# Graph network, residual layers and four norms on one core: opening and ending re-ordered, two norms of the ending moved to ScalarE

## The reference

```
for _ in range(3):                                  # L0: gated graph network, in_mat = out_mat = adj
    a  = adj @ h ; av = [a, a]
    z  = sigmoid(lin(av, w3) + lin(h, u3)) ; r = sigmoid(lin(av, w4) + lin(h, u3))
    hv = tanh(lin(av, w5) + lin(r * h, u5))
    h  = (1 - z) * h + z * hv
x = ln(x + h)                                       # norm 0
rel = adj.T * (x Wq)(x Wk)^T ; rel = rel / ||rel||  # L1: relation between nodes
x = ln(x + rel @ (x Wv))                            # norm 1
x = ln(x + (adj @ x) @ weight2 + bias2)             # L2, norm 2
x = ln(x + norm_adj @ (x @ weight3) + bias3)        # L3, norm 3
```

## Time and profile before

| | us |
|---|---|
| median of 3 runs | 1214.63 (1214.09 to 1214.99) |
| the profiled execution | 1214.77 |
| its span in the trace | 1212.9 |
| PE busy in the span | 1198.3 (99%) |
| DVE busy | 1002.6 (83%) |
| ACT busy | 655.7 (54%) |
| POOL busy | 191.7 (16%) |

### The profile page before, as it was taken

How to read it: one execution, slowest core, us unless ns; L and a number is a source line. 1 busy time by engine, 2 the same in 40 slices (tenths; PEclk the granted TensorE clock), 3 DMA queues, 4 the chain that set the end, 5 groups by cost and what they waited for, 6 DMA issues and landing times.

```text
span 1212.9 us, 21243 instructions
## 1 busy us (share of the span) xinstructions
PE 1198.3 (99%) x7454; PEld 1079.2 (89%) x7454; DVE 1002.6 (83%) x2220; ACT 655.7 (54%) x1179; POOL 191.7 (16%) x447
## 2 busy tenths in 40 slices
PE   9999999999999999999999999999999999999997
PEld 8789899898988989899898998989889898998896
DVE  7689788897878879788897888978789797885898
ACT  5455555555555555555555555555555555554442
POOL 1002021110211203012020211102111030120022
PEclk9999999999999999999999999999999999999998
DMA  6030221303113030220302213031130302200001
GB/s 209 18 88 18 70 71 35 104 0 88 50 35 104 0 104 35 52 87 14 107 17 69 69 35 104 0 87 52 35 104 0 104 35 51 87 12 24 1 2 35
DMA packets 105021, 66.93 MB, mean 55 GB/s; under 512 B 65690, under 2 KB 98468, under 8 KB 104996
## 3 DMA queue, kind: packets, MB, share of 16 engines
q1 hardware_dynamic: 104784, 66.08, 18.2%
q0 software_dynamic: 192, 0.52, 0.2%
q10 hardware_dynamic: 20, 0.01, 0.0%
HBM read 35.13 MB, written 23.07 MB: 48 GB/s over the span
## 4 chain that ended last, share of the span: by engine, by line
PE 97%; DVE 2%; POOL 0%; ACT 0%; issue 0%; DVEq 0%; POOLq 0%
PE b_ps L520 41%; PE f_ps L520 32%; PE f_ps L515 15%; PE b_ps L515 7%; PE f_ps L682 1%; PE b_ps L746 1%; PE b_ps L564 0%; PE f_ps L1057 0%; DVE f_stats L1683 0%; DVE hf_feat L1699 0%; DVE f_gate L1699 0%; DVE b_rh_lo L1725 0%; PE b_ps L579 0%; DVE b_ps L1720 0%; PE f_ps L589 0%
## 5 line engine op out<-in xcount | busy, mean ns | idle before, releaser
L428 POOL TENSOR_TENSOR b_var_eps<-b_moments,eps 128x2 f32<-128x2 f32 x120 | 34.7, 289 | 904.2 <-DVE b_moments L1690 904.2
L1120 ACT ACTIVATE f_cand<-f_ps,bias_c 128x512 f32<-128x512 f32 x66 | 45.4, 689 | 85.2 <-PE f_ps L520 85.2
L430 POOL TENSOR_TENSOR b_rstd<-b_var_eps,neg_half 128x2 f32<-128x2 f32 x120 | 88.0, 733 | 9.4
L1068 ACT ACTIVATE b_rh_hi<-b_ps 128x512 fp32r<-128x512 f32 x90 | 53.6, 596 | 63.0 <-PE b_ps L520 62.9
L1108 ACT ACTIVATE f_gate<-f_ps,bias_r 128x512 f32<-128x512 f32 x66 | 45.3, 686 | 71.0 <-PE f_ps L520 71.0
L1068 ACT ACTIVATE b_a_hi<-normed 128x512 fp32r<-128x512 f32 x60 | 37.8, 630 | 60.0 <-DVE normed L1699 60.0
L520 PE MATMUL f_ps<-adjT_hi,hf_node_hi 128*128 128x256 f32 x264 | 66.4, 285 | 0.0
L520 PE MATMUL f_ps<-adjT_lo,hf_node_hi 128*128 128x256 f32 x264 | 65.0, 280 | 0.0
L1582 DVE TENSOR_TENSOR f_cand<-f_z,f_cand 128x512 f32<-128x512 f32 x66 | 45.4, 688 | 23.0 <-ACT f_cand L1120 22.9
L1725 DVE TENSOR_TENSOR b_rh_lo<-b_ps,b_rh_hi 128x512 fp32r<-128x512 f32 x90 | 61.1, 679 | 4.0 <-ACT b_rh_hi L1068 3.9
L1566 DVE TENSOR_TENSOR f_gate<-f_gate,hf_feat 128x512 f32<-128x512 f32 x66 | 44.7, 678 | 20.0 <-ACT f_gate L1108 20.0
(11 more groups left out here) (340 smaller groups left out, 4304.4 us busy)
## 6 DMA issues: line engine op xcount, KB each, us to landing
x_front<-in_x SPq DMA_DIRECT2D x16, 512.0 KB, 3.9
x_blocks<-in_x SPq DMA_DIRECT2D x60, 128.0 KB, 2.9
input_t<-hf_feat SPq DMA_DIRECT2D x15, 512.0 KB, 3.0
turn_sum<-normed SPq DMA_DIRECT2D x14, 512.0 KB, 2.7
result<-turn_sum SPq DMA_DIRECT2D x56, 128.0 KB, 2.9
turn_f<-f_gate SPq DMA_DIRECT2D x14, 512.0 KB, 2.7
f_z<-turn_f SPq DMA_DIRECT2D x56, 128.0 KB, 2.8
out<-result SPq DMA_DIRECT2D x14, 512.0 KB, 3.2
```

Of the source, the lines that this page charges most:

```text
L428: pool.tensor_tensor(Y.var_eps[:, g], Y.moments[:, g, :, 1], eps[:], ALU.add).then_inc(Y.s_var, 1)
L430: pool.tensor_tensor(Y.rstd[:, g], Y.var_eps[:, g], neg_half[:], ALU.pow).then_inc(Y.s_rstd, 1)
L1068: return act.activation(dst, src, ACT.Copy)
L1120: act.activation(L.cand[:, k], L.ps1[:, k], ACT.Tanh, bias=bias_c[:, k:k + 1]).then_inc(L.s_tanh, 1)
```

## The change

The loop's `body` is as it was. Four things are changed.

1. **First back state, turned in the back lane's bank.** `turn_h(state_b, 0, k)` wrote `front.ps1`; it now writes `back.ps1` (`turn_bank`), and waits for `s_prep_lo` 8 (the preparation that used that bank). The mix of pair 1's first round, `mix(front, 2, k, 1)`, no longer waits for the turned state to be read, but for the tanh of the round before that reads the same bank, and stands ahead of the turning.
2. **Norms 1 and 2 of the ending on ACT.** `normalise` and the copy `conv_x_hi` go; ACT computes `x * rstd + shift` twice, once into `x_hi` (`layer_x_hi`) and once into the full-precision tile (`layer_normed`), from SBUF for norm 1 and from PSUM for norm 2. `conv_x_lo` and `fill` wait for the second. POOL adds `neg_mean` and `shift` for these norms.
3. **The hand-written orders of `start()`** on all engines.
4. **The hand-written orders of `finish()`**, with norm 3 of one graph applied ahead of the last statistics.

```diff
@@ norms
         def shifts(q, j, g):
-            return 8 * q + (4 if j == 3 else 0) + 2 * g + 2
+            return 8 * q + (4 if j >= 2 else 0) + 2 * g + 2
...
+        def turn_bank(S, v):
+            return back.ps1 if S is state_b and not later(v) else front.ps1
...
@@ POOL
             def inverse_std(Y, q, j, g, ending=False):
-                shifted = j in (0, 3) and not ending
+                shifted = j in ((1, 2) if ending else (0, 3))
...
@@ PE
-                if pair is not None and later(pair):
+                if pair is not None and isinstance(n, int) and n == 2:
+                    pe.wait_ge(front.s_tanh, upto(1, k))
+                elif pair is not None and later(pair):
                     pe.wait_ge(state_b.s_node_lo, upto(pair - 1, k))
...
             def turn_h(S, v, g):
                 pe.wait_ge(S.s_feat, upto(v))
-                turn(front.ps1, g, S.feat, S.s_turned)
+                if S is state_b and not later(v):
+                    pe.wait_ge(s_prep_lo, 8)
+                turn(turn_bank(S, v), g, S.feat, S.s_turned)
...
@@ PE, start()
                 candidate_reset(front, 1, 1)
+                for k in range(2):
+                    mix(front, 2, k, 1)
+                for k in range(2):
+                    turn_h(state_b, 0, k)
                 base(back, 0, 0)
                 for k in range(2):
-                    turn_h(state_b, 0, k)
+                    mix(back, 0, k, turned=True)
                 base(back, 0, 1)
...
@@ ACT
+            def layer_x(Y, q, j, g, dst):
+                for c in range(C):
+                    src = Y.normed[:, g, c] if j == 1 else Y.ps0[:, g, c * D:(c + 1) * D]
+                    last = act.activation(dst[:, g, c], src, ACT.Identity, bias=Y.shift[:, g, c:c + 1],
+                                          scale=Y.rstd[:, g, c:c + 1])
+                return last
+
+            def layer_x_hi(Y, q, j, g):
+                act.wait_ge(Y.s_shift, shifts(q, j, g))
+                layer_x(Y, q, j, g, Y.x_hi).then_inc(Y.s_x_hi, 1)
+
+            def layer_normed(Y, q, j, g):
+                act.wait_ge(Y.s_shift, shifts(q, j, g))
+                act.wait_ge(Y.s_x_hi, conv(q, j - 1, g))
+                layer_x(Y, q, j, g, Y.normed).then_inc(Y.s_normed, 1)
...
@@ DVE
-            def conv_x_lo(Y, q, j, g):
+            def conv_x_lo(Y, q, j, g, ending=False):
+                if ending:
+                    dve.wait_ge(Y.s_normed, mid(q, j + 1, g))
                 graph_lo(Y.x_lo, Y.x_hi, Y.normed[:, g], Y.s_x_hi, conv(q, j, g), g, Y.s_x_lo)
```

More of the change, by code:

```diff
@@ L942, in finish @@
-                for k in range(2):
-                    convolve(last_pair, 0, 0, k)
+                convolve(last_pair, 0, 0, 0)
+                mix_nodes(last_pair, 0, 0, 1)
                 mix_nodes(main, LAST - 1, 0, 1)
+                convolve(last_pair, 0, 0, 1)
+                convolve(main, LAST - 1, 0, 1)
                 mix_nodes(main, LAST - 1, 1, 0)
-                convolve(main, LAST - 1, 0, 1)
                 mix_nodes(last_pair, 0, 1, 0)
@@ L1906, in finish @@
[L1906 to L1909 removed]
                 new_sum(main, LAST - 1, LAST - 1, 0)
+                reset_h(front, 2 * LAST + 1, 1)
+                rh_lo(front, 2 * LAST + 1, 0)
                 keep(front, 2 * LAST + 1, 0)
+                rh_lo(front, 2 * LAST + 1, 1)
+                keep(front, 2 * LAST + 1, 1)
+                residual(main, back, LAST - 1, LAST - 1, 1)
@@ L1990, in finish @@
                 moments_of(last_pair, 0, 1, 1)
-                fill(last_pair, 0, 0, 0)
-                sum_attended(main, LAST - 1, 1)
-                normalise(last_pair, 0, 1, 1)
-                conv_ax_lo(main, LAST - 1, 0, 0)
-                stats_of(main, LAST - 1, 1, 1)
-                for k in range(2):
-                    conv_x_lo(last_pair, 0, 0, k)
+                sum_attended(main, LAST - 1, 1)
+                conv_x_lo(last_pair, 0, 0, 0, True)
+                stats_of(main, LAST - 1, 1, 1)
@@ L2189, in start @@
                 normalise(main, 0, 2, 0)
                 stats_of(main, 0, 2, 1)
-                prep_lo(10)
-                conv_x_lo(main, 0, 1, 0)
                 moments_of(main, 0, 2, 1)
+                keep(front, 3, 0)
+                rh_lo(front, 3, 1)
+                normalise(main, 0, 2, 1)
+                keep(front, 3, 1)
                 fill(main, 0, 1, 0)
-                keep(front, 3, 1)
-                normalise(main, 0, 2, 1)
-                candidate_part(front, 3, 0)
@@ L2198, in start @@
-                conv_x_lo(main, 0, 1, 1)
+                for k in range(2):
+                    conv_x_lo(main, 0, 1, k)
+                for k in range(2):
+                    candidate_part(front, 3, k)
                 hand_over_h(1, 0)
-                candidate_part(front, 3, 1)
                 conv_ax_lo(main, 0, 1, 0)
```

693 lines of the change are left out of this document (343 added, 350 removed).

## The result

The changed kernel takes 1208.09 us (median of 4 runs, 1207.88 to 1208.38), the kernel before 1214.81 beside it (4 runs, 1214.09 to 1216.31): a ratio of 0.9945 with a 95% interval of 0.993 to 0.996. The profiled execution took 1207.88 us, 6.9 less than that of before. 1206.4 was forecast: the direction and the three places were right, and the change brought 1.7 us less than the sum said. The time lies in the stated range (1204.2 to 1210.8), but above the forecast's own case, which ended at 1207.7.

A forecast was written before the change was run, and what follows sets the result against it. PE was taken to bound the kernel, except DVE in the last 16 blocks. Gains of 2.6 (opening), 4.8 (blocks) and 0.9 (tail), 8.3 us off 1214.77 and 0.14 for the median, gave 1206.4 us; range 1204.2 to 1210.8.

The forecast's parts named there:

- The gap in the opening: Opening, PE's waits for `hb_feat_hi`: two mixes moved into the gap fill it, a gain of 2.3 us.
- The two waits of 0.2: Head of the opening, PE's waits for `u3T_lo` and `f_a_lo`: new order covers them, gaining 0.3 of 0.4 us.
- The rest of the opening and the start of the ending: Re-ordered work outside the gaps stays dense: 0 us change, with +1.0 as the bound for each part.
- The last 16 blocks: Ending: relieving DVE takes the stretch from 29.2 to 24.4 us, a gain of 4.8; bounds 6.5 and 0.
- `neg_mean` and `shift` 0.46: Ending, chain behind each norm: POOL's two added operations take 0.46 us before ACT's pair into `x_hi`.
- I followed the first two blocks ... the next 0.2.: Ending: first `mix_nodes` waits 0.3 to 0.5 us for its low part, the next 0.2; 1.7 us of waits stay.
- DVE needs 22.7 us: Last 16 blocks: DVE's work falls from 27.97 to 22.7 us, no longer more than PE's 22.5.
- The clock: Ending: clock taken to stay at its upper level; as rival it falls, losing 1.7 us: 1208.1, chance 0.10.
- The tail: After PE's last matmul: one group of norm 3 less on DVE, a gain of 0.9 us; bounds 0.5 and 1.5.
- The longer chain eats the ending: Rival, ending: ACT's queue makes each of 16 blocks wait 0.25 us more, keeping 0.8 of 4.8: 1210.4, chance 0.14.
- the replaced wait: Rival, opening: new waits replace the old, so its 2.6 us gain becomes nearly 0: 1209.0, chance 0.07.
- the slower end: Rival, ending: `conv_x_lo` holds DVE's queue and all eight norms come late, losing 8.4 us: 1219.5, chance 0.07.

The follow-up runs named there:

- Experiment 3: Changed kernel, but on PE the turning of the first back state stands ahead of the two mixes, not behind them: 1211.0 us.
- the third chip's 1208.50: The changed kernel timed again with no edit, as the reference for the last three kernels: 1208.50 us.
- experiment 11: Changed kernel, but on DVE `conv_x_lo` of main's first graph stands ahead of last_pair's statistics, and the fill behind them: 1208.53 us.
- experiment 10: Changed kernel, but the four shifts of last_pair's norms one and two are computed by DVE in one operation each, not by POOL: 1207.74 us.
- experiment 4: Changed kernel and its orders, but norms one and two of the ending are normalised on DVE and copied by ACT again: 1211.96 us.
- experiment 7: Changed kernel, but the ending's fill copies the residual alone, without the bias, so it has one SBUF input, not two: 1207.10 us.
- experiment 12: Changed kernel with last_pair's shifts on DVE and `conv_x_lo` of main's first graph ahead, both edits together: 1207.64 us.
- experiment 8: Changed kernel, but norm 3 of main's first graph stands behind the last moments again, all four groups in the tail: 1209.11 us.
- experiment 5: Changed kernel, but on ACT the copy of mixed nodes (`b_rh_hi`) stands ahead of `layer_x_hi(last_pair, 0, 2, 1)`: 1207.95 us.
- Experiment 1: Opening as changed, ending (order, and norms one and two on DVE) as in the kernel before: 1210.86 us, ratio 0.9972.
- experiment 6: Changed kernel, but the negated mean in the ending is computed by DVE behind the moments, not by POOL: 1207.94 us.

## Why the prediction was right, and where it was off

**The gap in the opening (2.3 forecast): right.** All steps came as written: the second mix at 47.93, no wait for the tanh, the turning behind it. The margin of the turning was 0.4 us: the state was ready at 48.93. Experiment 3 takes only this back and loses about 2.8, with a wait of 2.3 us in its profile. Against the third chip's 1208.50 it would be 2.4, so the difference between the two can't be read more closely.

**The two waits of 0.2 (0.3 forecast): not settled.** Both are gone from the list, but 0.5 for `adjT_lo` is there in the changed kernel, none in experiment 11, 0.2 in experiment 10. The start of the program differs between executions. The first matmul of the ending stands at 1079.48 to 1080.56 in the eleven profiles with the new opening as changed, and at 1082.30 and 1082.47 in the two with the old one: 1.7 to 3.0 us, 2.4 between the means. The forecast of 2.6 lies inside.

**The rest of the opening and the start of the ending (0 forecast): right.** The start of the ending takes 93.93 us where it took 94.03; the rest of the opening has no row of its own and is inside the 2.4.

**The last 16 blocks (24.4 forecast, 26.28 measured): here the sum was off.** The mechanism was right: the move to ACT is worth 3.9 us (experiment 4), and DVE had been the bound. ACT's terms held: the pair from PSUM took 1.01 to 1.05 us where 1.0 was taken and the Trainium skill ("ScalarE: Activation LUTs", section "What ACT_TABLE_LOAD costs") led to an estimate of 1.03, the pair from SBUF 1.08 to 1.10, and ACT was busy 18.4 us in the stretch. Three sizes were not right:

- *"`neg_mean` and `shift` 0.46".* That was taken from a place where DVE was not in the way. In the ending they took from 0.46 to 1.32 us, 1.29 in the chain above. The step that failed is that the price of POOL's operations was read from one quiet spot. The hold also reached the first operation of the chain, which the sum took as unchanged: `f_var_eps` took 0.69 for 0.20. It is the largest miss: without the hold by the fill alone the stretch takes 25.17 (experiment 7), with the shift off POOL 25.22 (experiment 10). So 1.1 of the 1.9 us that were missing are here. No experiment ties down the other 0.8; the next point says where they show.
- *"I followed the first two blocks ... the next 0.2."* The chain of the first norm was followed to `b_a_lo` only. PE waits 0.58 there, 0.17 and 0.23 for the two `f_a_lo`, with a stretched matmul group behind each. In experiments 11 and 12 moving `b_a_lo` ahead did not shorten this part, since `f_a_lo` comes last: two activations in a row do not fit beside two blocks of PE, and in experiment 12 DVE's queue adds 0.4.
- *"DVE needs 22.7 us".* It was busy 24.03. One of the eight `normalise` pairs lay ahead of the stretch in the kernel before (1171.77), and more than half of a `fill` (1173.10 to 1173.79) lies in it that lay ahead before (1174.39, with the stretch from 1176.50). DVE's idle spots add to it, since operations that follow each other at once overlap in the records. DVE is idle 2.3 us all the same, so this cost nothing by itself.

The trace of the kernel before had the warning. POOL's first operation for `b_rstd`, and DVE's `fill` over the same time:

```profile
1184.33 0.55 POOL L428 TENSOR_TENSOR b_var_eps<-b_moments,eps 128x2 f32<-128x2 f32 x1 [4.14 <-DVE b_moments L1690]
```

```profile
1184.16 0.68 DVE L1720 TENSOR_TENSOR f_ps<-hf_feat,bias_out 128x512 f32<-128x512 f32 x1
```

It ends at 1184.88, 0.04 us behind the fill, where 0.20 is its usual length. Before the change no row shows a wait for it. The Trainium skill states the rule: a VectorE instruction with two SBUF inputs contends with a GpSimd instruction that reads SBUF ("SBUF — State Buffer", section "Who interferes with whom"), and the one that starts second is blocked until the first is done (same page, section "SBUF: two separate sides"). The rows here agree for POOL as the second, those with one input in PSUM too (experiment 7). They do not show the other half: where DVE is the second it keeps its usual time. In the changed kernel the fill at 1187.51 began while POOL's power ran (1187.06 to 1187.75) and took 0.68, and `f_a_lo` at 1194.61 began under another (1194.09 to 1195.24) and took 0.69.

**The clock (stays up, 1.7 us of the gain): right in kind.** It was 1.00 through the whole ending. With the same order the stretch takes 29.13 us with the fall and 27.92 without it, so the fall costs 1.2 where 1.7 was taken. Of the 2.85 us that the profiled pair shows, 1.2 are this, and 1.6 are left for the move and the new order, where the forecast's 4.8 left 3.1. The forecast also took the fall as a fixed part of the kernel before. It isn't: against the ten fastest of its 27 runs (1212.9 to 1214.0, mean clock 0.998 or 0.999) the changed kernel gains some 5.5 us and not 6.7. That the reference's median contains a lower clock is luck for the forecast.

**The tail (0.9 forecast): right,** 7.27 to 6.31 us, and 1.0 back in experiment 8.

**The rivals.** "The longer chain eats the ending" is what came in part: 1.9 of its 4.0 us. 1.1 of them go through ACT's queue as it said, but are set off by POOL. The clock, the replaced wait and the slower end did not come: no wait of the ending exceeded 0.95 us.

## What to carry to other kernels

- Price a moved operation where it will stand, not where it was found: look for the same form beside the neighbours it will get. In these traces a small POOL operation that began while DVE ran a 128x512 operation with two SBUF inputs was held until that ended, and a chain of four took 2.8 us instead of 1.5. If such a chain ends in something that an engine's stream waits for, try the small work on DVE itself: there the shift took 0.16 us in one operation (experiment 10).
- When a wait names a copy whose own input was long ready, look at what stands ahead of it in that engine's stream. Moving the copy moves the wait (experiment 5); shortening what the stream waits for removes it (experiment 10).
- A wait of PE can cost more than its length, because the clock may fall behind it in some of the runs. The spread narrowed as well: the changed kernel's nine runs lie within 0.9 us, the 49 of the kernel before within 3.9.

## What the runs showed of the hardware

- Whether the granted clock falls behind the same wait differs from run to run. Experiment 1 and the kernel before run the same ending, one at 1.00 and one at 0.67 over the same 5 us of it. Behind one wait of 2.3 us it was 0.50 in the profile of experiment 3, with matmuls 0.21 us apart until 52.9, and five of that kernel's eight runs have a time without such a loss. What decides it is open.
- A held POOL operation of 0.20 us ends 0.03 to 0.06 us behind the DVE operation that holds it. The power (`f_rstd`, `b_rstd`), 0.69 us alone, is held too and ends 0.55 us behind: in experiment 6 it took 1.01 us, to 1188.44, and `b_a_lo` had ended at 1187.89; in the changed kernel 1.15, to 1195.24, behind 1194.69.
- The hold goes one way here. In the endings of all fourteen profiles, the 128x512 operations of DVE with two SBUF inputs that began while a POOL operation ran took 0.67 to 0.70 us, as they do alone.
